# Two TensorE stages of the chunk loop joined into one, and two VectorE stages joined into one, in a delta-rule attention kernel

## The reference, cut to what matters

```python
def t_step(M, kv):
    Mk = jnp.einsum('bhde,bhe->bhd', M, k_t)
    forget = Mk[..., :, None] * k_t[..., None, :]
    write = v_t[..., :, None] * k_t[..., None, :]
    return (M - alpha * forget + beta * write, None)

def chunk_step(M, qkv):
    scores = jnp.einsum('bhid,bhjd->bhij', qi, ki) * scale
    scores = jnp.where(mask, -jnp.inf, scores)
    attn = jax.nn.softmax(scores, axis=-1)
    attn_out = jnp.einsum('bhij,bhjd->bhid', attn, vi)
    mem_out = jnp.einsum('bhid,bhde->bhie', qi, M)
    chunk_out = attn_out + 0.1 * mem_out
    M, _ = jax.lax.scan(t_step, M, kv)
    return (M, chunk_out)
```

## Time and profile before

| | |
|---|---|
| time, median of 3 runs | 6047.22 us (6035.39 to 6054.13) |
| the profiled execution's own time | 6053.87 us |
| span of its slowest core, shown here | 6052.3 us |
| spans of all 8 cores | 6021.6 to 6052.3 us |
| TensorE busy, share of the span | 34% |
| VectorE busy | 30% |
| ScalarE busy | 23% |
| TensorE clock granted, mean over the span | 0.563 of full speed |

### The profile page before, as it was taken

The page is one execution under the profiler, slowest core; times in us unless marked ns, Lnnn a source line. Parts: engine busy times, 40 slices in busy tenths (PEclk is TensorE's granted clock), DMA queues, the critical chain, the costliest instruction groups (busy, mean ns, idle before and its releaser), DMA issues.

```text
span 6052.3 us, 67280 instructions; the slowest of 8 cores (6021.6 to 6052.3 us)
## 1 busy us (share of the span) xinstructions
PE 2064.3 (34%) x28902; PEld 1254.1 (21%) x28902; DVE 1813.2 (30%) x2294; ACT 1408.3 (23%) x1443; POOL 59.9 (1%) x85
## 2 busy tenths in 40 slices
PE   1433433433433433433433434222243222223422
PEld 0232232232232232232232133000121000001200
DVE  2243243243243243243243243222222012222210
ACT  1211311221221211211221221333332013333300
POOL 0000000000000000000000000000000000000000
PEclk9556656655655655655655655555555555555555
DMA  4000000000000000000000000000175420004744
GB/s 71 1 1 21 1 1 21 1 1 21 1 1 22 1 1 22 1 1 22 1 1 19 3 1 2 15 7 7 20 121 109 112 64 9 7 7 82 119 105 113
DMA packets 92213, 172.36 MB, mean 28 GB/s; under 512 B 5824, under 2 KB 38672, under 8 KB 87824
## 3 DMA queue, kind: packets, MB, share of 16 engines
q1 hardware_dynamic: 44032, 125.84, 7.6%
q0 software_dynamic: 47888, 42.21, 5.4%
HBM read 151.44 MB, written 58.72 MB: 35 GB/s over the span
## 4 chain that ended last, share of the span: by engine, by line
PE 34%; DVE 22%; ACT 20%; DMA 16%; issue 8%; DVEq 1%; SPq 0%; ACTq 0%; POOLq 0%
DMA x1t_sb<-x1d 6%; PE psB L437 4%; PE psB L405 3%; PE psC L411 3%; ACT L418 3%; ACT L734 3%; DVE A L451 3%; PE pb L724 3%; PE psB L325 2%; PE psA L312 2%; PE psC L325 2%; ACT B L418 2%; DMA interd<-inter_sb 2%; PE psA L586 2%; PE pb L815 2%
## 5 line engine op out<-in xcount | busy, mean ns | idle before, releaser
L405 PE MATMUL psB<-A,B 64*64 64x64 bf16 x5120 | 272.6, 238 | 490.1 <-ACT B L418 386.0
L418 ACT ACT_TABLE_LOAD x128 | 164.2, 1283 | 926.0 <-PE psC L411 926.0
L405 PEld LDWEIGHTS psB<-A,B 64*64 64x64 bf16 x5120 | 255.8, 151 | 507.0 <-issue 507.0
L420 DVE CAST A<-psB 128x1024 bf16<-128x1024 f32 x160 | 195.8, 1224 | 524.5 <-PE psC L411 441.4
L734 ACT ACT_TABLE_LOAD x128 | 164.2, 1283 | 565.1 <-PE pb L724 565.1
L789 DVE CAST inter_sb<-pb 128x1024 bf16<-128x1024 f32 x128 | 154.2, 1222 | 436.8 <-DMA interd<-inter_sb 247.2
L486 ACT ACT_TABLE_LOAD x64 | 82.1, 1283 | 852.8 <-PE psC L481 852.8
L325 PE MATMUL psB<-wk_sb,xn_fm 128*128 128x512 bf16 x512 | 183.5, 446 | 254.9 <-DVE kb_tm L353 246.6
L724 PE MATMUL pb<-psel_sb,y_sb 128*128 128x512 bf16 x256 | 149.9, 585 | 348.9 <-ACT sel_sb L734 202.4
L437 PE MATMUL psB<-A 64*64 64x64 bf16 x5120 | 170.2, 238 | 273.8 <-DVE A L451 219.0
L815 PE MATMUL pb<-f1a,pselT_sb 128*128 128x512 bf16 x256 | 112.7, 619 | 418.9 <-DMA x1t_sb<-x1d 418.9
(11 more groups left out here) (162 smaller groups left out, 4597.0 us busy)
## 6 DMA issues: line engine op xcount, KB each, us to landing
interd<-inter_sb SPq DMA_DIRECT2D x32, 1024.0 KB, 9.4
f1a<-interd SPq DMA_DIRECT2D x32, 1024.0 KB, 7.7
x_sb<-x SPq DMA_DIRECT2D x16, 1024.0 KB, 7.0
x1t_sb<-x1d SPq DMA_DIRECT2D x64, 256.0 KB, 5.2
f<-f2w POOLq DMA_DIRECT2D x32, 512.0 KB, 5.5
out<-outf_sb SPq DMA_DIRECT2D x32, 512.0 KB, 2.6
x1d<-x_sb SPq DMA_DIRECT2D x16, 512.0 KB, 3.6
f1a<-f1w POOLq DMA_DIRECT2D x16, 512.0 KB, 10.8
```

Source lines behind the costliest of these rows:

```text
L405: sq_fns.append(lambda t, k=k, h=h, par=par: t.matmul(psB[par:par + 64, h * 64:h * 64 + 64], B_bufs[k][par:par + 64, h * 64:h * 64 + 64], ...
L418: E("s", [lambda s, k=k: s.copy(B_bufs[k + 1][:], psC[:, 0:1024])], waits={"t": tS})
L420: vM = E("v", [lambda v, k=k: v.tensor_copy(A_bufs[k + 1][:], psB[:, 0:1024])], waits={"t": tS})
```

## The change

The 32 matmuls of `tHM` are put in the same stage as those of `tPV`, behind them. The joined stage waits for `vR` and `sE`, and both names hold the count at its end. On VectorE the steps of H and M are put in the same stage as the output sum; that stage now carries the wait for `tHM` and the wait for VectorE's own count.

```diff
                                     v_tm[pbase:pbase + 64, tl * 1024 + h * 64:tl * 1024 + h * 64 + 64],
                                     start=True, stop=True, tile_position=(pbase, pbase)))
-                            tPV = E("t", fns, waits={"v": vP, "s": sE})
-                            fns = []
                             for h in range(NH):
                                 hr = (h % 2) * 8 + h // 2
                                 wsl = W_fin[b][pbase:pbase + 64, hr * 64:hr * 64 + 64]
...
-                            tHM = E("t", fns, waits={"v": vR})
+                            tPV = tHM = E("t", fns, waits={"v": vR, "s": sE})
                             vRe = E("v", [lambda v, pbase=pbase: v.reciprocal(
                                 re_sb[pbase:pbase + 64, 0:16], psD[pbase:pbase + 64, 0:16])],
                                 waits={"t": tPV})
...
-                            ], selfdep=True)
-                            E("v", [
                                 lambda v, b=b: v.tensor_add(
                                     H_sb[:, b * 512:(b + 1) * 512],
...
-                            ], waits={"t": tHM})
+                            ], waits={"t": tHM}, selfdep=True)
```

## The result

| | before | after |
|---|---|---|
| median of 8 runs | 6046.38 us (6028.63 to 6054.93) | 6175.55 us (6165.18 to 6182.23) |
| ratio after to before | | 1.0217, 95% interval 1.0201 to 1.0232 |
| span of the slowest core in the profiled execution | 6052.3 us | 6174.1 us |
| mean granted TensorE clock of that core | 0.563 | 0.561 |

The changed kernel is 2.2% slower, 129 us by the medians. The forecast was 2.0% and 6167 us, with a range of 6138 to 6196. A ninth run of the changed kernel, not among the eight of the table, took 6158.74 us; it changes nothing in this.

The account below looks back on a forecast made before the run. The kernel was taken as a string of hand-overs between engines without slack, so 0.78 + 1.09 = 1.87 us a pass, times 64, gave 119.7 us: 6167 us, 2.0% slower, range 6138 to 6196 us.

Parts of the forecast that it names:

- Part 1: First matmul of `tPV` on TensorE waits for RHS_sb (L503) instead of L495: starts 0.78 us later each pass.
- Rival 3: First matmul of `tPV` isn't later, because VectorE doesn't set its start: 70 us slower, 6117 us; chance 0.05.
- Part 2: VectorE's reciprocal waits for 64 matmuls instead of 32: 1.09 us later each pass, at 34 ns a matmul of `tHM`.
- rival 1: Matmuls of `tHM` are as short as their records: reciprocal only 0.86 us later a pass, 6152 us; chance 0.15.
- rival 2: Matmuls of `tHM` go one by one: reciprocal 1.70 us later a pass, 6206 us; chance 0.10.
- Part 3: Branch and wait removed on TensorE and on VectorE between L544 and the H step: nothing gained, at most 6 us.
- rival 4: TensorE gets its faster clock in the passes from one uninterrupted stretch of 64 matmuls: 22 us faster, 6025 us; chance 0.03.
- Rival 5: The change does nothing because the compiled order hides it: 6047 us; chance 0.02.

Follow-up runs that it names:

- part 3 alone: Only the two VectorE stages (output sum, steps of H and M) joined, against the kernel before: 6047.31 us against 6044.61, ratio 1.0006.

## Why the prediction was right, point by point

- **The pass has no slack and each loss comes 64 times: shown.** Losses of 0.79 and 1.11 us and a gain of 1.19 a pass add up over 64 passes to 51, 71 and 76 us, and the runs moved by 51, 82 and 75 us. In the changed kernel too the M step released TensorE 64 times.
- **Part 1, 0.78 us: right.** 0.79 measured alone, and the 0.26 us hand-over holds behind L503 as behind L495. Rival 3 (the start isn't VectorE's) is out. Why the hand-over takes 0.26 us here and 0.14 us ahead of `tSMm` (the prediction: because two engines are waited for) no run tests; keeping the 0.26 was enough.
- **Part 2, 1.09 us: right, a little small.** 1.11 measured alone and 1.13 in the pass shown; over 64 passes that is 1 to 3 us too little in the sum. The prices of rivals 1 and 2 are out. The reason given, semaphore counts taken one after another, was only argued in the prediction; the runs with one count per burst show it. They also correct it in one thing. The prediction held that the modelled ends come too early and that a matmul here costs 34 ns. The modelled ends fit: with one count the waiter follows them. So rival 1 had the array right, its matmuls are as short as their records, and only left out the counts; the 34 ns belong to the count, not to the matmul.
- **Part 3, nothing: right for the changed kernel.** In the pass shown the H step still starts before L542 ends (1277.99 against 1278.07); in the passes of the second chunk there never was such an overlap, and there too nothing changed. The bounds, 0 to 6 us faster, missed that the joined stage could also be slower by a second wait, as in the run with part 3 alone (4.3 us in the trace).
- **The clock, rival 4: out.** 0.50 in the passes. The groups of matmuls were gapless before, so joining their stages changes nothing that TensorE does. Rival 5, no change, is out with 129 us.
- **The size.** The sum was 119.7 us; the profile shows 122.1 in the passes and 121.8 between the spans; the medians of 8 runs are 129 us apart, 122 to 140 by the interval. What lies between the trace and the medians I could not place.

## What to carry to other kernels

Where engines hand work to each other without slack, a stage boundary with its own wait isn't overhead, it is what lets the next engine begin: before joining two stages, ask what the earlier one released and what the later one waited for, and price the join at both (here 0.79 us for waiting too soon and 1.11 us for being told too late, 64 times). The same look shows where to split: the mask was all that `tPV` needed, and letting it go first made the kernel before 1.3% faster. And when every one of a burst of short instructions raises a semaphore, measure from the burst's start to the waiter: if the waiter starts well after the modelled end of the last matmul, raise it once, by the last. This holds for bursts whose last instruction also ends last, as the modelled ends have it here.

## What the runs showed of the hardware

- A count raised by a matmul takes about 34 ns, and counts queue. The lag of the last one is about the number of matmuls times (34 ns less the spacing of the matmuls). Measured, as the difference between many counts and one: 32 at 27 ns lag 0.22 us (1.39 to 1.17), 64 at 27 ns 0.48 us (2.49 to 2.01), 48 at 27 ns 0.38 us (1.95 to 1.57), 32 at 13 ns (all 32 within 0.64 us) 0.64 us (1.40 to 0.76), 32 at 53 ns none. The product gives 0.22, 0.45, 0.34, 0.67 and none. The Trainium skill (TensorE: Matmul & The Clock Gate, section "The cost: per-tile semaphore tail") names the mechanism; its tail has 26.3 ns for each increment, 4.7 ns for each tile and 25 ns once, and no term for the spacing. In these runs the lag grows only where matmuls come faster than the counts: the 32 of `tPV` have no tail that one count would remove.
- With one count, a burst's waiter starts 0.09 to 0.10 us behind the modelled end of the last matmul where it is VectorE (1.07 us of burst, 1.17 to the waiter), and 0.06 to 0.07 us where it is ScalarE. So the modelled ends fit these bursts, and the late waiter of many counts was no sign against them.
- A second semaphore to wait for cost VectorE 0.07 us ahead of L544, though it had been reached before (11.0 against 6.7 us of idle time over 64 passes).
